# Two-layer graph network on one core: index copies on ScalarE, messages written by columns, 16-bit destination blocks

## The chip, the core and the metric

The kernel runs on one core of a Trainium2 chip. The metric is the device time of one execution in microseconds (us). The engines are PE (matmul), PEld (its weight loads), DVE (VectorE), ACT (ScalarE), POOL (GpSimd) and SP (SyncE, which here only issues DMAs). All 16 DMA engines serve all queues.

## The reference

There are 12500 nodes with 32 features and 200000 edges sorted by destination. Cut to what matters:

```python
# layer 0: a message per edge, summed over the edges of a destination
xs = concat(x[src, :8], x[dst, :8]); xv = concat(x[src, 8:], x[dst, 8:])      # 16 scalars, 16 3-vectors
h = 2.0 ** 0.5 * relu(emb @ W1 / 10.0 ** 0.5)
w = (h @ W2 / 16.0 ** 0.5).reshape(E, 7, 16, 8)                               # weights of each edge
s_out, g_out, v_out = (einsums of xs, xv, the edge's direction, and w)        # 8, 8 and 8x3
message = concat(G * tanh(s_out), G * tanh(g_out)[:, :, None] * v_out) * norm  # 32 numbers, G = 1.593
x = layernorm(x + segment_sum(message, dst))
# layer 1: attention over the edges of each destination
e = leaky_relu((x @ a1)[src] + (x @ a2)[dst])
x = layernorm(x + segment_sum(x[src] * softmax_by_dst(e), dst))
```

## The kernel before

Edges lie on 125 partitions, 1600 to each (EP = 1600), so a column is 125 edges. The kernel has three large stages and short ones between and behind them.

**The first stage (0 to about 378 us)** finds where each node's edges begin and end in the sorted list of destinations. The destinations come in as int32 (dst_i); DVE casts them to f32 (L332, dstf) and ACT stores them to DRAM as dstf_d, 500 blocks of 400 (L455 and the lines about it). A coarse search compares each node's number with the first entry of every block (L361 on DVE, L464 on ACT). For the fine search POOL gathers, for each of the 100 nodes of a partition, the right block of 400 destinations into one of NF = 8 buffers of blkbuf (L302, an indirect DMA), and DVE counts the entries that are at most the node's number (L381, one tensor_scalar with an accumulator). POOL may issue gather k when L381 has finished k - 8. Before these, POOL waits for the permuted features xp in DRAM (DVE L354 and L355, then ACT's store), gathers one row per head of a partition (L281) and 32 columns of source rows early (L287); behind the block gathers come 8 more columns, one small gather (L306) and 100 scatters of node rows to xd_d (L312). The message stage starts when these have landed. SP in the meantime writes 25.6 MB of zeros to xd_d and loads the edges' vectors.

**The message stage (378 to 2584 us)** goes over the 1600 columns in 200 pieces of 8 (PW = 8), 5 pieces to a chunk of 40 columns, 10 pieces (RING) to a turn of the loop. POOL gathers the source rows of each column into edge (L628), ten pieces ahead: when ACT has finished high(p) (semaphore b_hi), the slot of piece p is free and the gathers of piece p + 10 go into it. As the loop's piece is a register, POOL first copies the 8 index columns from src_i to idx (L625), waits for its own copy, and issues 8 gathers with columns of idx. The first turn takes src_i itself.

Per piece DVE projects the vectors on the edge's direction (two L865, one L870), ACT's function high places the features for PE (three copies at L673 and L674, into HL), PE transposes them (L758), ACT copies the result out (L680, FT), PE computes the hidden layer (L783; ACT relu, L684) and three pairs of products (L763), and DVE multiplies them by the hidden layer (L880, six per piece, 1000 columns each). PE sums (L792), ACT copies out (L688, rt), PE transposes back (L803, Y_ps), ACT takes tanh (L692, th), and DVE's function post makes the messages: L894 (pa), L899 (pg, the gates), L900 (the 8 scalars into O), L903 (pb), and later, between the second and third multiply of a step, L906 (the 24 vector entries into O). O is stored feature by feature, each of the 32 features with 41 columns (C1 = 41), because four scans over columns (L921) sum it by destination. pb lies as column, then 24 entries; pg as column, then 8; th as column, then 16. Each group of 4 columns is a step; the order of all these on an engine is written out by hand in the functions turn. Four more scans (L851) spread node rows over the edges, and ACT copies them in and out (L648, L660, L666). SP loads a chunk's inputs and stores its sums.

**The second layer (2780 to 4340 us)** looks rows up by one-hot matmuls on PE and by gathers on POOL. Two lines of DVE outside of the message stage serve as yardsticks: L1119 subtracts two tables of 26 x 33 entries, one of which it reads with 33 words from element to element while it writes runs; L1422 multiplies 40 rows of 32 and writes them 41 words apart.

```python
ov = cols(O[h])[:, 1 + c0:1 + c0 + PW, :]
V.tensor_tensor(ov[:, :, 8:32].rearrange("p c (w a) -> p c w a", a=3), pbv,
                pgv.rearrange("p c (w a) -> p c w a", a=1).broadcast_to([P, PW, MO, 3]), ALU.mult)
```

Of the kernel before, what the change touches and what calls it, by code (L numbers as in the profile page):

```python
# [5 lines left out]
def gnn_resnorm_kernel(nc, x, src, dst, emb, vec, weight, W1, W2, attn, out):  # L6
    f32 = mybir.dt.float32
    f32r = mybir.dt.float32r
    i32 = mybir.dt.int32
# [84 lines left out]
    with ctx:  # L94
# [7 lines left out]
            return nc.dram_tensor(name, shape, dt, kind="Internal").ap()  # L102


        dstf_d = dram("dstf_d", (NSB, SB))
        end_d = dram("end_d", (N + 1, 1))
        xd_d = dram("xd_d", (E, DIM))
        sd_d = dram("sd_d", (E, 1))
# [39 lines left out]
        R_ps = ctx.enter_context(nc.psum_tensor("R_ps", [128, 512], f32))  # L148
        Y_ps = ctx.enter_context(nc.psum_tensor("Y_ps", [128, 512], f32))

        src_i = sb("src_i", [PG, EP], i32)
        idx = sb("idx", [PG, RING * PW], i32)
        edge = sb("edge", [PG, RING * PW * EW])
        edge_c = edge[:, :].rearrange("p (c f) -> p c f", f=EW)
# [11 lines left out]
        with ExitStack() as st:  # L166
# [2 lines left out]

            dst_i = sbt("dst_i", [P, EP], i32)  # L170
            dstf = sbt("dstf", [P, EP + 1])
            prev_i = sbt("prev_i", [P, 1], i32)
            keep = sbt("keep", [P, EP])
            dirv = sbt("dirv", [P, EP * 3])
# [12 lines left out]
            cnt = sbt("cnt", [P, NP])  # L187
            blk_i = sbt("blk_i", [PG, NP], i32)
            fine = sbt("fine", [P, NP])
            blkbuf = sbt("blkbuf", [PG, NF * SB])  # L190
            w2s = sbt("w2s", [HID, 7 * 128])
            zeros = sbt("zeros", [PG, ZW])
            w2x = sbt("w2x", [HID, NR * MO * NQ * KF])
# [17 lines left out]
            with nc.Block() as block:  # L211
                @block.sync
                def _(sp):
                    by_rows(sp, dst_i[:, :], edges(dst, 1), S("a_dst"))
                    sp.wait_ge(S("a_idxz"), 2)
                    by_rows(sp, src_i[0:P, :], edges(src, 1), S("a_src"))
                    sp.dma_start(prev_i[1:P, :], dst.rearrange("(p c) -> p c", c=EP)[0:P - 1, EP - 1:EP], allow_slow_non_contiguous=True).then_inc(S("a_prev"), 16)
                    sp.wait_ge(S("a_zero"), 1)
                    sp.wait_ge(S("a_tab"), 32)
                    for i in range(NZ):  # L220
                        sp.dma_start(xd_d.rearrange("e f -> (e f)").rearrange("(p w) -> p w", p=PG)[:, i * ZW:(i + 1) * ZW], zeros[:, :]).then_inc(S("a_xd0"), 16)
                    sp.dma_start(end_d[0:1, :], zeros[0:1, 0:1]).then_inc(S("a_end"), 16)
                    sp.dma_start(w2s[:, :], W2).then_inc(S("a_w"), 16)
                    sp.dma_start(attn_b[:, :], attn.rearrange("(a f) -> a f", a=1).broadcast_to([P, 2 * DIM])).then_inc(S("a_w"), 16)
                    sp.wait_ge(S("a_wh0"), 1)
                    for row, k0, k1 in ((2 * KF + 8, 0, 8), (2 * KF + 24, 8, NEMB)):
                        sp.dma_start(w1x[row:row + k1 - k0, :].rearrange("k (w j) -> k w j", j=HID),
                                     W1[k0:k1, :].rearrange("k (w j) -> k w j", w=1).broadcast_to([k1 - k0, MO, HID])).then_inc(S("a_w1"), 16)
                    by_rows(sp, dirv[:, :], vec.rearrange("(p c) f -> p (c f)", c=EP), S("a_vec"))
                    sp.dma_start(sd_d.rearrange("e a -> (e a)").rearrange("(p w) -> p w", p=64), zeros[0:64, 0:E // 64]).then_inc(S("a_pad"), 16)  # L230
                    sp.dma_start(y0_d[E:E + PAD, :].rearrange("(a b) f -> a (b f)", a=64), zeros[0:64, 0:4 * DIM]).then_inc(S("a_pad"), 16)
                    sp.dma_start(y1_d[E:E + PAD, :].rearrange("(a b) f -> a (b f)", a=64), zeros[0:64, 0:4 * R1]).then_inc(S("a_pad"), 16)

                    sp.wait_ge(S("a_endf"), 1)
                    by_rows(sp, end_d[1:N + 1, :].rearrange("(p k) a -> p (k a)", k=NP), endf[:, :], S("a_end"))
                    sp.wait_ge(S("a_end"), 48)
                    by_rows(sp, startf[:, :], end_d[0:N, :].rearrange("(p k) a -> p (k a)", k=NP), S("a_start"))
                    sp.wait_ge(S("a_keep"), 1)
                    by_rows(sp, keep_d.rearrange("(p c) -> p c", c=EP), keep[:, :], S("a_out"))
                    sp.wait_ge(S("a_dir"), 1)  # L240
                    by_rows(sp, dir_d.rearrange("(p c) f -> p (c f)", c=EP), dirv[:, :], S("a_out"))
                    for a in range(2):
                        sp.wait_ge(S("a_selt"), a + 1)
                        sp.dma_start(sel_d[a].rearrange("(b r) p -> r b p", b=4), selT[a][:, :].rearrange("r (b p) -> r b p", b=4)).then_inc(S("a_out"), 16)
                    sp.wait_ge(S("a_out"), 96)
                    sp.wait_ge(S("a_pad"), 48)

                @block.gpsimd
                def _(pool):
# [47 lines left out]
                    for k in range(NP):  # L297
                        if k % NPH == 0:
                            pool.wait_ge(S("a_blk"), k // NPH + 1)
                        if k >= NF:  # L300
                            pool.wait_ge(S("a_fine"), k - NF + 1)
                        nc.gpsimd.indirect_dma_start(out=blkbuf[:, (k % NF) * SB:(k % NF + 1) * SB], out_offset=None, in_=dstf_d,  # L302
                                                     in_offset=bass.IndirectOffsetOnAxis(blk_i[:, k:k + 1], 0)).then_inc(S(f"a_fg{k % NF}"), 16)
                    early(EARLY - 1)
                    pool.wait_ge(S("a_start"), 32)
# [15 lines left out]
                def _(dve):  # L321
# [8 lines left out]
                    V.memset(zeros[:, :], 0.0).then_inc(S("a_zero"), 1)  # L330
                    dve.wait_ge(S("a_dst"), 32)
                    V.tensor_copy(dstf[:, 1:], dst_i[:, :]).then_inc(S("a_dstf"), 1)  # L332
                    dve.wait_ge(S("a_dstf"), 1)
                    dve.wait_ge(S("a_id"), 2)
                    V.tensor_tensor(blkbuf[0:P, 0:NSB].rearrange("p (j q) -> p j q", q=P),
# [41 lines left out]
                    for k in range(NP):  # L377
                        dve.wait_ge(S(f"a_fg{k % NF}"), 16 * (k // NF + 1))
                        if k >= NF:
                            dve.wait_ge(S("a_fine"), k - NF + 1)  # L380
                        V.tensor_scalar(junk[:, (k % NF) * SB:(k % NF + 1) * SB], blkbuf[0:P, (k % NF) * SB:(k % NF + 1) * SB], nodef[:, k:k + 1], None,  # L381
                                        ALU.is_le, ALU.add, accum_out=fine[:, k:k + 1]).then_inc(S("a_fine"), 1)
                    dve.wait_ge(S("a_fine"), NP)
                    V.scalar_tensor_tensor(endf[:, :], tn[:, 0:NP], float(SB), fine[:, :], ALU.mult, ALU.add).then_inc(S("a_endf"), 1)
# [55 lines left out]
                    step(V.tensor_copy(ssel[:, 0:E0], src_i[0:P, 0:E0]))  # L440
                    for pos in range(NB):
                        step(V.tensor_copy(ssel[:, E0:E0 + ITERS * XCB].rearrange("p (u c) -> p u c", c=XCB)[:, :, sum(XCS[:pos]):sum(XCS[:pos + 1])],
                                           src_i[0:P, :].rearrange("p (u h c) -> p u h c", h=NB, c=C)[:, :, pos, CGS[pos]:C]))
                    step(V.tensor_scalar(psel[:, :], ssel[:, :], 1.0 / KL, -(KL - 1) / (2.0 * KL), ALU.mult, ALU.add))
                    step(V.tensor_scalar(psel[:, :], psel[:, :], MAGIC, None, ALU.add))
                    V.tensor_scalar(psel[:, :], psel[:, :], -MAGIC, None, ALU.add).then_inc(S("a_sel"), 1)
# [3 lines left out]
                @block.scalar  # L450
                def _(act):
                    by_rows(act, xn[:, :], x.rearrange("(p k) f -> p (k f)", k=NP), S("a_x"))
                    act.wait_ge(S("a_dstf"), 1)
                    act.sem_inc(S("go"), 1)
                    by_rows(act, dstf_d.rearrange("a b -> (a b)").rearrange("(p c) -> p c", c=EP), dstf[:, 1:], S("a_dstd"))  # L455
                    act.wait_ge(S("a_xp"), 2)
                    act.sem_inc(S("go"), 1)
                    by_rows(act, xp_d.rearrange("(p k) f -> p (k f)", k=NP), xp[0:P, :], S("a_tab"))
# [38 lines left out]
        with ExitStack() as st:  # L497
# [58 lines left out]
            with nc.Block() as block:  # L556
# [51 lines left out]
                def _(pool):  # L608
# [8 lines left out]
                    def turn(t):  # L617
                        fixed = isinstance(t, int)
                        for s in range(RING):
                            p = t * RING + s  # L620
                            for c in range(PW):
                                pace(p, c)
                                i = s * PW + c
                                if c == 0 and not fixed:
                                    nc.gpsimd.tensor_copy(idx[:, i:i + PW], src_i[:, bass.ds((p + RING) * PW, PW)]).then_inc(S("b_ix"), 1)  # L625
                                    hold(S("b_ix"), p - RING + 1)
                                col = src_i[:, (p + RING) * PW + c:(p + RING) * PW + c + 1] if fixed else idx[:, i:i + 1]
                                nc.gpsimd.indirect_dma_start(out=edge_c[:, i, 8:8 + DIM], out_offset=None, in_=xp_d,  # L628
                                                             in_offset=bass.IndirectOffsetOnAxis(col, 0)).then_inc(S(f"b_gx{s}"), 16)
# [9 lines left out]
                def _(act):  # L639
# [25 lines left out]
                            act.wait_ge(S("b_st"), ch * 32)  # L665
                        A.activation(zr[:, :].rearrange("p (c f) -> p c f", f=DIM)[:, :, i * 8:(i + 1) * 8], cols(Z[h])[:, 1:, i * 8:(i + 1) * 8], ACT.Copy).then_inc(S("b_zr"), 1)  # L666

                    def high(p, s, ch):
                        act.wait_ge(S("b_al"), p + 1)
                        if s % PC == 0:  # L670
                            act.wait_ge(S("b_em"), ch * 2 + 2)
                        for d in range(2):
# [22 lines left out]
                    def turn(t, first=False, last=False):  # L695
                        for g in range(G2):
# [3 lines left out]
                                out_of_R(t * RING + g // 2 - 2)  # L700
                            if k == 0 and not (last and g + 4 >= G2):
                                s = (g + 4) // 2
                                high(t * RING + s, s % RING, t * 2 + s // PC)
                            if not (last and h == 1):
                                if gc == 0:
                                    place_emb(ch + 1, 1 - h, t + h)
# [130 lines left out]
                def _(dve):  # L837
# [48 lines left out]
                    def post(i, m, h, q, t):  # L886
                        c0 = q * PW
                        nrm = nmp[h][:, c0:c0 + PW].rearrange("p (c w) -> p c w", w=1).broadcast_to([P, PW, MO])
                        ov = cols(O[h])[:, 1 + c0:1 + c0 + PW, :]
                        if i == 0:  # L890
                            if q == 0:
                                dve.wait_ge(S(f"b_lp{h}"), t * 96 + 96)
# [4 lines left out]
                            if some(m):  # L897
                                dve.wait_ge(S("b_o"), m)
                            V.scalar_tensor_tensor(pgv, thv[:, :, 8:16], TG, nrm, ALU.mult, ALU.mult).then_inc(S("b_gs"), 1)  # L899
                            V.scalar_tensor_tensor(ov[:, :, 0:8], thv[:, :, 0:8], TG, nrm, ALU.mult, ALU.mult).then_inc(S("b_gs"), 1)  # L900
                        if i == 1:
                            dve.wait_ge(S("b_pa"), m + 1)
                            V.tensor_tensor(pbv, pav, yv[:, :, KF:KF + 24].rearrange("p c (a w) -> p c w a", a=3), ALU.add).then_inc(S("b_yr"), 1)  # L903
                        if i == 2:
                            dve.wait_ge(S("b_yr"), m + 1)
                            V.tensor_tensor(ov[:, :, 8:32].rearrange("p c (w a) -> p c w a", a=3), pbv,  # L906
                                            pgv.rearrange("p c (w a) -> p c w a", a=1).broadcast_to([P, PW, MO, 3]), ALU.mult).then_inc(S("b_o"), 1)

                    def carry_sums(ch, h, t):
                        if not isinstance(t, int) or t + h > 0:  # L910
# [663 lines left out]
```

## Time and profile before

| | us |
|---|---|
| median of 3 runs (lowest, highest) | 4478.09 (4477.6, 4480.03) |
| the profiled execution's own time | 4480.86 |
| its span | 4479.1 |
| first stage, from the span's start to | 378 |
| message stage | 378 to 2584 |
| between the layers | 2584 to 2780 |
| second layer | 2780 to 4340 |
| last sums and normalization | 4340 to 4479 |

The span reaches from the first to the last instruction; 1.8 us of the execution lie outside it. Idle time in the views is listed with what ended it. A line's mean is over instructions of one form where the view says "by form".

### The profile page before, as it was taken

The page shows a single profiled execution, that of the slowest core. Times are in us where ns is not written, and L with a number is a line of the kernel's source. Part 1 is how long each engine was busy: PE and PEld are TensorE (multiplying, and loading weights), DVE is VectorE, ACT ScalarE, POOL GpSimd, SP SyncE. Part 2 cuts the span into 40 slices and gives each one's busy share as a digit, 9 for nine tenths or more (in the row PEclk, how much of TensorE's full clock was granted, in tenths as well). Part 3 has the DMA queues.
Part 4 walks back from the last instruction along what each step waited for, and adds up shares of the span by engine and source line. Part 5 has one row for each costly group of instructions (what it writes and reads, how often), then busy time and mean ns, then how long its engine had stood idle before and what let it go on. Part 6 is the DMA issues. An engine that isn't in the chain of part 4 may idle for free. (4 is left out here: it accounts for less than half of the span.)

```text
span 4479.1 us, 67002 instructions
## 1 busy us (share of the span) xinstructions
PE 3332.8 (74%) x20487; PEld 2103.2 (47%) x20487; DVE 3036.9 (68%) x5225; ACT 2154.7 (48%) x4565; POOL 3247.6 (73%) x3440
## 2 busy tenths in 40 slices
PE   0003888888888888888888802999999999999940
PEld 0001332332332333233323202899999999999940
DVE  4433999999999999999999833344444444444432
ACT  3002555555555555555555310466666666666620
POOL 5776777777777777777777467777777777777766
PEclk9999999999999999999999955999999999999975
DMA  9612222222222222222222112133333333333311
GB/s 334 164 45 45 40 47 49 52 46 47 46 46 47 50 53 47 46 47 46 47 49 52 22 29 56 39 68 77 73 82 74 75 72 73 72 73 72 73 30 26
DMA packets 271192, 283.33 MB, mean 63 GB/s; under 512 B 182593, under 2 KB 236073, under 8 KB 268403
## 3 DMA queue, kind: packets, MB, share of 16 engines
q1 hardware_dynamic: 164150, 207.75, 16.8%
q0 software_dynamic: 106528, 70.98, 10.3%
q10 hardware_dynamic: 462, 4.00, 0.3%
q8 instruction: 21, 0.34, 0.0%
q14 instruction: 31, 0.25, 0.0%
HBM read 192.06 MB, written 90.42 MB: 63 GB/s over the span
## 5 line engine op out<-in xcount | busy, mean ns | idle before, releaser
L628 POOL DMA_INDIRECT edge<-xp_d,idx x1440 | 1420.8, 987 | 537.5 <-issue 393.6
L880 DVE TENSOR_TENSOR prod<-G_ps,hid 128x1000 f32<-128x1000 f32 x1200 | 1399.9, 1194 | 125.6 <-PE G_ps L763 111.3
L1275 POOL DMA_INDIRECT x1e<-tab_d,idxb x1122 | 1100.0, 980 | 342.2 <-issue 337.9
L763 PE MATMUL G_ps<-FT,wst 32*128 32x500 f32 x4800 | 896.6, 633 | 371.0 <-DVE prod L880 367.8
L1324 PE MATMUL G_ps<-tb,hot 128*126 128x442 f32 (+1 forms) x3968 | 799.1, 358 | 0.3 <-DVE x1e L1349 0.2
L1324 PEld LDWEIGHTS G_ps<-tb,hot 128*126 128x126 f32 x3968 | 743.0, 187 | 37.8 <-DVE x1e L1349 1.4
L763 PEld LDWEIGHTS G_ps<-FT,wst 32*128 32x128 f32 x4800 | 246.3, 183 | 807.4 <-DVE prod L880 750.7
L792 PE MATMUL R_ps<-prod,red 128*32 128x500 f32 x4800 | 590.5, 595 | 0.0
L684 ACT ACTIVATE hid<-T_ps 128x500 f32<-128x500 f32 x400 | 233.5, 584 | 721.5 <-PE T_ps L783 688.9
L1324 PE MATMUL T_ps<-tb,hot 128*126 128x442 f32 x2000 | 416.2, 360 | 186.3 <-DVE one_d L1408 186.3
L1324 PEld LDWEIGHTS T_ps<-tb,hot 128*126 128x126 f32 x2000 | 376.6, 188 | 204.9 <-issue 186.4
L783 PE MATMUL T_ps<-FT,wst 32*128 32x500 f32 x800 | 432.3, 619 | 3.1 <-ACT FT L680 3.1
L1349 DVE TENSOR_REDUCE x1e<-G_ps 125x17 f32<-125x442 f32 x496 | 269.9, 597 | 196.9 <-PE G_ps L1324 191.7
L758 PE MATMUL T_ps<-ident,HL 125*128 125x125 f32 x1600 | 250.1, 279 | 130.0 <-ACT HL L674 129.9
L1295 ACT ACTIVATE sqb<-x1e,sqb 125x32 f32<-125x32 f32 x1560 | 336.9, 341 | 0.0
L1324 PE MATMUL R_ps<-tb,hot 128*126 128x442 f32 x840 | 310.9, 370 | 16.9 <-DVE x1e L1349 16.9
L673 ACT ACTIVATE HL<-edge 125x384 f32<-125x384 f32 x400 | 187.3, 515 | 276.3 <-DVE edge L870 276.2
L792 PEld LDWEIGHTS R_ps<-prod,red 128*32 128x32 f32 x4800 | 115.6, 109 | 414.0 <-issue 266.3
L758 PEld LDWEIGHTS T_ps<-ident,HL 125*128 125x128 f32 x1600 | 177.3, 142 | 282.5 <-issue 149.9
L1324 PE MATMUL Y_ps<-tb,hot 128*126 128x416 f32 x840 | 300.0, 357 | 0.0
L1040 ACT ACTIVATE ab<-edge,niot 128x1375 f32<-128x1375 f32 (+2 forms) x172 | 245.4, 1451 | 74.1 <-PE Y_ps L1324 35.9
L1290 ACT ACTIVATE sqb<-ex 125x40 f32<-125x40 f32 x40 | 9.5, 239 | 527.9 <-DVE one_d L1381 527.9
(235 smaller groups left out, 4369.5 us busy)
## 6 DMA issues: line engine op xcount, KB each, us to landing
xd_d<-zeros SPq DMA_DIRECT2D x16, 1562.5 KB, 28.6
y_d<-ng SPq DMA_DIRECT2D x40, 595.0 KB
edge<-xp_d,idx POOLq DMA_INDIRECT x1440
xv<-xd_d SPq DMA_DIRECT2D x40, 560.0 KB
y_d<-zr SPq DMA_DIRECT2D x40, 560.0 KB
x1e<-tab_d,idxb POOLq DMA_INDIRECT x1122
edge<-sel_d SPq DMA_DIRECT2D x20, 750.0 KB
edge<-sel_d SPq DMA_DIRECT2D x20, 687.5 KB
```

The lines of the kernel that those rows point to most:

```text
L628: nc.gpsimd.indirect_dma_start(out=edge_c[:, i, 8:8 + DIM], out_offset=None, in_=xp_d, in_offset=bass.IndirectOffsetOnAxis(col, 0)).then_i ...
L684: A.activation(hid[k][:, :], T_ps[1][:, 0:GW], ACT.Relu, scale=HSCALE).then_inc(S("b_hid"), 1)
L758: last = Tn.transpose(T_ps[0][:, c * P:(c + 1) * P], HL[g // 2 % 2][:, col0:col0 + HW], ident[0:P, 0:P])
L763: return Tn.matmul(G_ps[pair][:, a * 512:a * 512 + GW], wst[rows, r * 128:(r + 1) * 128], FT[k][rows, :], start=True, stop=True)
L783: Tn.matmul(T_ps[1][:, 0:GW], wst[2 * KF:3 * KF, 128:256], FT[k][2 * KF:3 * KF, :], start=True, stop=True).then_inc(S("b_H"), 1)
L792: last = Tn.matmul(R_ps[32 * q:32 * q + 32, 0:GW], red[:, u * KF:(u + 1) * KF], prod[b * 2 + q // 2][pair][:, a * GW:(a + 1) * GW], start= ...
L880: V.tensor_tensor(prod[b][i][:, :].rearrange("p (a e) -> p a e", a=2), gv, hid[k][:, :].rearrange("p (a e) -> p a e", a=1).broadcast_to([1 ...
L1040: nc.scalar.activation(ab[g % 2][:, 0:w], nodek[b][:, 0:w] if g == NG4 - 1 else nodes[b][:, 0:w], ACT.Abs, bias=niot[:, g:g + 1]).then_inc ...
L1275: nc.gpsimd.indirect_dma_start(out=gx[b][:, c * T1:(c + 1) * T1], out_offset=None, in_=tab_d, in_offset=bass.IndirectOffsetOnAxis(idx[b][: ...
L1295: last = nc.scalar.activation(wxv[:, 1 + c, 0:DIM], gx[h][0:P, c * T1:c * T1 + DIM], ACT.Copy, scale=wx[:, DIM * C1 + 1 + c:DIM * C1 + 2 + c])
L1324: last = nc.tensor.matmul(ps[0:PE2, 0:w], hot[b][:, g * XPM + j * P:g * XPM + j * P + PE2], tb[l][:, g * GS + f0 * KL:g * GS + f0 * KL + w ...
L1349: V.tensor_reduce(gx[b][0:P, c * T1 + f0:c * T1 + f1], ps[0:P, 0:(f1 - f0) * KL].rearrange("p (f k) -> p f k", k=KL), AX.X, ALU.max).then_ ...
```

## The change

POOL no longer copies index columns. ACT does it in high, after its wait for DVE's projection and before its own three copies, for the pieces whose gathers the loop issues; POOL's wait for b_hi covers it. src_i is 16 columns wider, since ACT in its last full turn copies two pieces beyond the end. The two DVE instructions that write O run feature by feature with the columns innermost. In the first stage a second cast makes int16 destinations (dst16), they are what is stored and gathered (blk16), and DVE compares them in that form; blkbuf remains for the coarse search and two small tables.

```diff
-        dstf_d = dram("dstf_d", (NSB, SB))
+        dst16_d = dram("dst16_d", (NSB, SB), mybir.dt.int16)
...
-        src_i = sb("src_i", [PG, EP], i32)
+        src_i = sb("src_i", [PG, EP + 2 * PW], i32)
...
-            blkbuf = sbt("blkbuf", [PG, NF * SB])
+            blkbuf = sbt("blkbuf", [PG, 8 * P])
+            blk16 = sbt("blk16", [PG, NF * SB], mybir.dt.int16)
...
-                        nc.gpsimd.indirect_dma_start(out=blkbuf[:, (k % NF) * SB:(k % NF + 1) * SB], out_offset=None, in_=dstf_d,
+                        nc.gpsimd.indirect_dma_start(out=blk16[:, (k % NF) * SB:(k % NF + 1) * SB], out_offset=None, in_=dst16_d,
...
                     V.tensor_copy(dstf[:, 1:], dst_i[:, :]).then_inc(S("a_dstf"), 1)
+                    V.tensor_copy(dst16[:, :], dst_i[:, :]).then_inc(S("a_dstf"), 1)
...
-                        V.tensor_scalar(junk[:, (k % NF) * SB:(k % NF + 1) * SB], blkbuf[0:P, (k % NF) * SB:(k % NF + 1) * SB], nodef[:, k:k + 1], None,
+                        V.tensor_scalar(junk[:, (k % NF) * SB:(k % NF + 1) * SB], blk16[0:P, (k % NF) * SB:(k % NF + 1) * SB], nodef[:, k:k + 1], None,
...
-                    act.wait_ge(S("a_dstf"), 1)
+                    act.wait_ge(S("a_dstf"), 2)
                     act.sem_inc(S("go"), 1)
-                    by_rows(act, dstf_d.rearrange("a b -> (a b)").rearrange("(p c) -> p c", c=EP), dstf[:, 1:], S("a_dstd"))
+                    by_rows(act, dst16_d.rearrange("a b -> (a b)").rearrange("(p c) -> p c", c=EP), dst16[:, :], S("a_dstd"))
...
-                                if c == 0 and not fixed:
-                                    nc.gpsimd.tensor_copy(idx[:, i:i + PW], src_i[:, bass.ds((p + RING) * PW, PW)]).then_inc(S("b_ix"), 1)
-                                    hold(S("b_ix"), p - RING + 1)
...
-                    def high(p, s, ch):
+                    def high(p, s, ch, fetch=False):
                         act.wait_ge(S("b_al"), p + 1)
+                        if fetch:
+                            A.activation(idx[:, s * PW:(s + 1) * PW], src_i[:, bass.ds((p + RING) * PW, PW)], ACT.Copy)
...
-                                high(t * RING + s, s % RING, t * 2 + s // PC)
+                                high(t * RING + s, s % RING, t * 2 + s // PC, not last and not (first and s < RING))
...
-                        ov = cols(O[h])[:, 1 + c0:1 + c0 + PW, :]
+                        of = O[h][:, :].rearrange("p (f c) -> p f c", c=C1)[:, :, 1 + c0:1 + c0 + PW]
...
-                            V.scalar_tensor_tensor(ov[:, :, 0:8], thv[:, :, 0:8], TG, nrm, ALU.mult, ALU.mult).then_inc(S("b_gs"), 1)
+                            V.scalar_tensor_tensor(of[:, 0:8, :], thv[:, :, 0:8].rearrange("p c w -> p w c"), TG,
+                                                   nmp[h][:, c0:c0 + PW].rearrange("p (w c) -> p w c", w=1).broadcast_to([P, MO, PW]),
+                                                   ALU.mult, ALU.mult).then_inc(S("b_gs"), 1)
...
-                            V.tensor_tensor(ov[:, :, 8:32].rearrange("p c (w a) -> p c w a", a=3), pbv,
-                                            pgv.rearrange("p c (w a) -> p c w a", a=1).broadcast_to([P, PW, MO, 3]), ALU.mult).then_inc(S("b_o"), 1)
+                            V.tensor_tensor(of[:, 8:32, :].rearrange("p (w a) c -> p w a c", a=3), pbv.rearrange("p c w a -> p w a c"),
+                                            pgv.rearrange("p c (w a) -> p w a c", a=1).broadcast_to([P, MO, 3, PW]), ALU.mult).then_inc(S("b_o"), 1)
```

## Rows read from the trace of the kernel before

**Rows 1.** The page, busy us of the whole span.

```profile
PE 3332.8 (74%) x20487; PEld 2103.2 (47%) x20487; DVE 3036.9 (68%) x5225; ACT 2154.7 (48%) x4565; POOL 3247.6 (73%) x3440
```

**Rows 2.** Windows: stretch, length, busy us of each engine, PEclk, DMA share, GB/s.

```profile
378.00:2584.00 2206.00, 1808.71 (x12800) 656.96 (x12800) 2060.16 (x3207) 1144.81 (x2361) 1583.03 (x1740) 1.00 0.23 47
...
70.80:122.40 51.60, 0.00 (x0) 0.00 (x0) 11.09 (x35) 0.00 (x0) 22.66 (x24) 1.00 0.99 326
122.40:217.00 94.60, 0.00 (x0) 0.00 (x0) 50.03 (x161) 0.00 (x0) 71.72 (x76) 1.00 0.61 166
```

**Rows 3.** Waits, 1000 to 2000 us: total us, times, longest us.

```profile
PEld G_ps L763 <- DVE prod L880: 365.6, 365, 1.4
ACT hid L684 <- PE T_ps L783: 312.8, 145, 4.4
...
POOL edge L628 <- POOL idx L625: 70.7, 90, 0.8
...
DVE prod L880 <- PE G_ps L763: 41.4, 105, 1.0
```

**Rows 4.** One line: xcount, ns min/median/max, first and last start us; last row, L865's waits.

```profile
L302 POOL DMA_INDIRECT blkbuf<-dstf_d,blk_i x100: 943/949/963, 70.8 to 216.4; - x100
...
L381 DVE TENSOR_SCALAR_CACHE_REDUCE junk<-blkbuf,nodef x100: 625/629/631, 79.5 to 219.5; 125x400 bf16<-125x400 f32 x100
...
L625 POOL COPY idx<-src_i x174: 196/202/831, 601.4 to 2524.8; 128x8 int32 x174
...
L906 DVE TENSOR_TENSOR O<-pb,pg x184: 498/509/585, 609.4 to 2579.5; 125x192 f32<-125x192 f32 x184
...
  DMA edge<-xp_d,idx: 1.0, 1
```

**Rows 5.** Timeline, message stage: start us, length us, engine, line.

```profile
1512.84 0.26 ACT L692 ACTIVATE th<-Y_ps 125x128 f32<-125x128 f32 x1
...
1513.72 0.35 DVE L894 TENSOR_TENSOR pa<-Y_ps,drp 125x192 f32<-125x192 f32 x1
...
2535.00 0.94 POOL L628 DMA_INDIRECT edge<-xp_d,idx  x1 [0.30 <-issue]
```

**Rows 6.** Timeline, first stage: in brackets the idle time before.

```profile
12.81 1.00 DVE L332 CAST dstf<-dst_i 125x1600 f32<-125x1600 int32 x1 [8.60 <-DMA dst_i<-in_dst]
...
27.86 1.39 POOL L281 DMA_INDIRECT hx_keep<-xp_d,head_i  x1 [18.70 <-DMA xp_d<-xp]
...
201.35 0.95 POOL L302 DMA_INDIRECT blkbuf<-dstf_d,blk_i  x1 [0.30 <-DVE junk L381]
```

**Rows 7.** ACT by line and form, 560 to 4479 us: busy us, mean ns.

```profile
L1290 ACT ACTIVATE sqb<-ex 125x40 f32<-125x40 f32 x40 | 9.5, 239 | 527.9 <-DVE one_d L1381 527.9
```

**Rows 8.** DVE by line and form, 560 to 4479 us: busy us, mean ns.

```profile
L880 DVE TENSOR_TENSOR prod<-G_ps,hid 128x1000 f32<-128x1000 f32 x1115 | 1300.8, 1194 | 102.6 <-PE G_ps L763 89.6
...
L870 DVE TENSOR_REDUCE edge<-tmp 125x128 f32<-125x384 f32 x183 | 105.5, 576 | 1.3
L906 DVE TENSOR_TENSOR O<-pb,pg 125x192 f32<-125x192 f32 x188 | 96.9, 515 | 0.1
...
L903 DVE TENSOR_TENSOR pb<-pa,Y_ps 125x192 f32<-125x192 f32 x188 | 65.1, 346 | 0.0
...
L900 DVE SCALAR_TENSOR_TENSOR O<-th,nmp 125x64 f32<-125x64 f32 x188 | 50.8, 270 | 0.0
L899 DVE SCALAR_TENSOR_TENSOR pg<-th,nmp 125x64 f32<-125x64 f32 x188 | 40.8, 217 | 0.0
...
L1119 DVE TENSOR_TENSOR tb<-tbl,tb 128x858 fp32r<-128x858 f32 x4 | 6.6, 1697 | 17.4 <-ACT tb L1151 17.4
...
L1422 DVE TENSOR_TENSOR sqb<-x1e,sqb 125x1280 f32<-125x1280 f32 x1 | 2.5, 2464 | 0.0
```

**Rows 9.** DMA queues, 80 to 90 us: packets, MB, share of 16 engines.

```profile
q1 hardware_dynamic: 298, 3.33, 78.6%
q0 software_dynamic: 294, 0.91, 22.5%
```

More of the change, by code:

```diff
@@ L171, in gnn_resnorm_kernel @@
             dstf = sbt("dstf", [P, EP + 1])
+            dst16 = sbt("dst16", [P, EP], mybir.dt.int16)
             prev_i = sbt("prev_i", [P, 1], i32)
@@ L215, in _ @@
                     sp.wait_ge(S("a_idxz"), 2)
-                    by_rows(sp, src_i[0:P, :], edges(src, 1), S("a_src"))
+                    by_rows(sp, src_i[0:P, 0:EP], edges(src, 1), S("a_src"))
                     sp.dma_start(prev_i[1:P, :], dst.rearrange("(p c) -> p c", c=EP)[0:P - 1, EP - 1:EP], allow_slow_non_contiguous=True).then_inc(S("a_prev"), 16)
@@ L442, in _ @@
                         step(V.tensor_copy(ssel[:, E0:E0 + ITERS * XCB].rearrange("p (u c) -> p u c", c=XCB)[:, :, sum(XCS[:pos]):sum(XCS[:pos + 1])],
-                                           src_i[0:P, :].rearrange("p (u h c) -> p u h c", h=NB, c=C)[:, :, pos, CGS[pos]:C]))
+                                           src_i[0:P, 0:EP].rearrange("p (u h c) -> p u h c", h=NB, c=C)[:, :, pos, CGS[pos]:C]))
                     step(V.tensor_scalar(psel[:, :], ssel[:, :], 1.0 / KL, -(KL - 1) / (2.0 * KL), ALU.mult, ALU.add))
```

## The prediction

> **What bounds the kernel now.** I began with the page [rows 1]: over the whole span PE, DVE and POOL are each busy about 70%, which is a mean over stages with different limits. So I cut the span into stages [rows 2]. The message stage (378 to 2584 us, half of the run) is the one the change mostly edits: DVE is busy 2060 of 2206 us, 93%, while PE has 82%, POOL 72% and ACT 52%. The table of waits says what the other 7% is [rows 3]: in 1000 us DVE waited 41 us for PE's G_ps, and PE waits for DVE many times longer. DVE's own work sets this stage.
>
> The share of POOL misleads, though. From 600 us on, its index copy starts first at 601.4 and, 173 copies later, at 2524.8 [rows 4]: 11.12 us per piece of 8 columns. DVE's L906, also once per piece, goes from 609.4 to 2579.5 in 183 steps: 10.77 us. POOL is slower than DVE by 0.35 us per piece and lives off its lead of ten pieces. The lead is just used up at the end: the last gather issues at 2535.0 [rows 5], and DVE waits for gathered rows once, 1.0 us [rows 4]. POOL is at the edge of being the bound, and costs 1 us now.
>
> The first stage ends with POOL too. One queue runs through it: early gathers, 100 gathers of destination blocks (70.8 to 216.4 [rows 4]), then 100 scatters; the message stage begins behind them. Where nothing holds it up, a block gather costs POOL 0.95 us plus 0.30 before the next [rows 6], 1.25 us; 99 steps want 124.2 us and took 145.6, so 21.4 us are stalls. They lie before 122.4, where the DMA engines are 99% busy; later they are 61% busy and POOL runs at its own pace [rows 2].
>
> **The change part by part, and the sum.**
>
> *Index copies, POOL to ACT.* Off POOL go 180 copies with the wait behind each: 0.20 us [rows 4] plus 70.7/90 = 0.79 us [rows 3], about 1 us per piece. POOL then needs some 10.1 us and waits for ACT's HL instead; no one waits for POOL. Worth: the 1.0 us at the end. ACT gets 180 copies of 8 columns. Nearest row: 239 ns for 40 columns [rows 7]; I take 0.2 us for 8, bounds 0 and 0.24. Each stands after the wait for DVE's L870 and ahead of HL, so everything queued behind it (HL, the copies of ds or xv, tanh, relu) starts 0.2 us later. The tightest cover I found is tanh to L894 in a piece with ds copies: tanh starts at 1512.84 for 0.26 us, L894 at 1513.72, 0.6 us to spare [rows 5]. Relu's own start is set by PE (313 us of waits in 1000 [rows 3]), which leaves ACT room ahead of it. I put it at 0; with the cover gone it would be up to 180 x 0.24 = 43 us. POOL's copies sharing SBUF with DVE: L906's mean is 515 and its median 509 [rows 4, 8], so their end is worth 0 to 1 us; I take 0. Nothing moves to or from SP's queue.
>
> *Messages along the columns.* Now L900 and L906 write O with a step of 41 words per element and read in runs. After it they write runs of 8 columns, and the reads step: L906 reads pb every 24 words and pg every 8, L900 reads th every 16 (nmp in a run). What do such steps cost? Two DVE rows without any (L880 with 1000 elements in 1194 ns, L903 with 192 in 346) give 1.05 ns per element and 144 ns fixed [rows 8]. A strided write, from the same rows: L906 is 169 ns above L903 of the same size, 0.88 per element; L1422 (1280 elements, writes 41 words apart) is 976 ns above the line, 0.76. A strided read: L1119 reads one of its two sources 33 words apart and writes in runs; 858 elements should take 1045 ns and take 1697, so 0.76 per element. A far step thus costs the same on a read as on a write, and the edit exchanges one for the other. With one such charge L906 becomes 346 + 192 x 0.76 = 492 ns, 23 less, x 200 pieces = -4.6 us. L900 becomes 217 + 64 x 0.76 = 266, 4 less; it stands where DVE next waits for PE, so 0. Between multiply 1 and multiply 2, where L906 stands, DVE doesn't wait, so it counts in full.
>
> Both of L906's sources step, however, and no row has that. Lower end: steps on reads almost free. L870 reads 384 elements 8 words apart in 576 ns against 547 by the line, 0.08 per element; so 361 ns, -154, -31 us. Upper end: two charges add, 346 + 2 x 0.76 x 192 = 638 ns, +123, +24.6 us. I take one charge, since L1119 is nearest (two sources, DVE, SBUF) and L870 has but one source.
>
> The Trainium skill's "Vector Engine (DVE) Microarchitecture Reference", section 5.2, speaks against this edit: two sources hopping per element cost little more than one (1.76 against 1.73 ns per column), but both stepping 24 words cost 2.50. The first figure agrees with the 1.81 of L1119; by the second, L906 would be an estimated 624 ns and the edit would lose 22 us. Rival A has that outcome with a price from rows.
>
> *16-bit destination blocks.* Each gather brings 128 rows of 800 B instead of 1600. DVE issues one more cast, ahead of the coarse search and of xp; L332, the same cast to f32, is 1.0 us [rows 6]. It lies ahead of everything up to xp, which DVE works off without a gap that could hide it, and POOL's queue starts at 27.86, when xp_d has landed [rows 6]; so +1.0, bounds 0.5 to 1.8, and behind it POOL and the whole stage shift. ACT's store of the blocks waits for the second cast too, but is not needed before 70.8, and halved it gets out of xp_d's way. The comparison L381 (629 ns [rows 4]) fits within POOL's 1.25 at either width: 0. Steady pace doesn't change either, since POOL sets it.
>
> The gain is in the 21.4 us of stall. From 80 to 90 us q1 (the zeros) and q0 (the gathers) take turns, 298 and 294 packets, 11.2 and 3.1 KB each [rows 9]. Halving the small packet of such a pair shortens it by 1.5 of 14.3 KB, about 10%; were there also fewer packets, it would be up to half. By bytes alone, q0's share of 22.5% would halve. Both ends: 0 and 21.4; I take a third, 7 to 8 us. Less the cast: -7.
>
> Sum: -7 (first stage), -4.6 (L906), -1.0 (POOL's wait) = -12.6. The profiled execution took 4480.9, 1.8 of it outside the span; it becomes 4468.3. The median of the runs is 2.8 below it, so 4478.1 - 12.6 = **4465.5 us**.
>
> **The rivals.**
>
> A, other side: the two strided reads of L906 add up, 638 ns. +24.6 - 7 - 1 = +16.6, 4494.7. For: pb and pg are distinct SBUF sources, both step at every element, and a writing step alone already costs 0.88. Against: only that no row shows it. Break-even is +40 ns (L906 at 555); from 600 ns it is slower by over 0.2%.
>
> B: reads in this order are cheap, 361 ns. -31 - 7 - 1 = -39, 4439. For: L870. Against: L1119. Only here does POOL's relief matter: at 11.12 us per piece it couldn't follow, at 10.1 it can.
>
> C: the 16-bit blocks don't shorten the stalls, because packets and not bytes are what takes turns. +1 - 4.6 - 1 = -4.6, 4473.5: the edit does not do what it says.
>
> D: ACT's copy shows up in DVE's waits for tanh. +20 to +43 on top, about 4500.
>
> **How the numbers follow.** Forecast 0.36, A 0.30, B 0.14, C 0.14, D 0.06. About 0.2% (9 us, 4469 to 4487) is what a measurement of this kernel can tell from no change. Faster: three quarters of the forecast's case, B, and a little of C = 0.43. Same: the rest of the forecast, most of C, a tail of A = 0.23. Slower: A and D = 0.34. The range goes from B, 4440, to just beyond A, 4500; with cases of both signs, the likeliest one's own range is 4455 to 4474 (stall gain 0 to 18).
>
> **What would show it.** L906 at about 490 ns, L900 near 266: right; 600 or more: A; below 400: B. The block gathers' span 138 us instead of 145.6, start 1.0 later. No L625; POOL idle before L628 named ACT HL, some 0.6 us per piece; DVE's waits for edge gone, and for tanh still below 10 us. Piece pace 10.75 instead of 10.77. The forecast is wrong if L906 is more than 40 ns above 515, or if the scatters begin no earlier.

## The result and the profile after

The changed kernel takes 4507.85 us (4501.05 to 4509.06) against 4477.85: 30.0 us more, ratio 1.0063, 95% interval 1.0048 to 1.0078. I forecast 12.6 us less. Times are medians; one execution of e12 below ran in a slower state of the chip (5017 us) and is left out of its median. The two profiled executions, stage by stage, by the first or last instruction of each stage:

| stretch | before, us | after, us | difference |
|---|---|---|---|
| to POOL's first gather of the message stage | 378.6 | 370.4 | -8.2 |
| message stage, to DVE's last copy (2583.1, 2605.2) | 2204.5 | 2234.8 | +30.3 |
| from there to L1119/L1123 (2763.7, 2785.8) | 180.6 | 180.6 | 0 |
| second layer, to the last gathers' start (4337.5, 4365.3) | 1573.8 | 1579.5 | +5.7 |
| the rest | 141.6 | 141.1 | -0.5 |

The first stage gained what was forecast and the message stage lost more than all of it. The 5.7 us of the second layer stand in code that nobody edited; over all the kernels of this study that stretch took 1573.8 to 1580.7 us, without a pattern, and I don't count it.

The windows of the kernel after (length, busy us of PE, PEld, DVE, ACT, POOL, PE clock, DMA share, GB/s), to be read beside [rows 2]:

```profile
71.70:115.00 43.30, 0.00 (x0) 0.00 (x0) 12.10 (x38) 0.00 (x0) 25.52 (x27) 1.00 0.97 333
115.00:210.00 95.00, 0.00 (x0) 0.00 (x0) 49.60 (x158) 0.00 (x0) 69.09 (x74) 1.00 0.33 86
370.00:2606.00 2236.00, 1803.94 (x12800) 656.14 (x12800) 2102.65 (x3203) 1162.05 (x2543) 1560.80 (x1560) 1.00 0.23 46
```

DVE is still the busy engine of the message stage, 2103 of 2236 us. The lines of DVE by form (total and mean ns; line numbers have moved: L910 is L906 of before, L902 is L900, L907 is L903, L901 is L899, L872 is L870, L882 is L880), beside [rows 8]:

```profile
L882 DVE TENSOR_TENSOR prod<-G_ps,hid 128x1000 f32<-128x1000 f32 x1112 | 1295.3, 1192 | 94.4 <-PE G_ps L765 78.0 <-issue 1.0
...
L910 DVE TENSOR_TENSOR O<-pb,pg 125x192 f32<-125x192 f32 x188 | 114.4, 609 | 0.1
...
L872 DVE TENSOR_REDUCE edge<-tmp 125x128 f32<-125x384 f32 x183 | 105.3, 575 | 1.3
...
L907 DVE TENSOR_TENSOR pb<-pa,Y_ps 125x192 f32<-125x192 f32 x187 | 64.2, 344 | 0.0
...
L902 DVE SCALAR_TENSOR_TENSOR O<-th,nmp 125x64 f32<-125x64 f32 x187 | 47.7, 255 | 0.0
L901 DVE SCALAR_TENSOR_TENSOR pg<-th,nmp 125x64 f32<-125x64 f32 x187 | 40.5, 217 | 0.0
```

L910 takes 609 ns for 515, L902 255 for 270; the rest stands. In durations that is 200 x (94 - 15) ns = 16 us, half of the 30. The other half is seen only in the timeline (start us, length us, engine, line). Before:

```profile
1506.95 0.55 DVE L906 TENSOR_TENSOR O<-pb,pg 125x192 f32<-125x192 f32 x1
1507.34 1.18 DVE L880 TENSOR_TENSOR prod<-G_ps,hid 128x1000 f32<-128x1000 f32 x1
```

After:

```profile
1505.65 0.61 DVE L910 TENSOR_TENSOR O<-pb,pg 125x192 f32<-125x192 f32 x1
1506.18 1.19 DVE L882 TENSOR_TENSOR prod<-G_ps,hid 128x1000 f32<-128x1000 f32 x1
```

DVE starts its next instruction before the last one has ended, so an instruction's length is not what it costs. What it costs is the time to the next start, here called its slot: 0.39 us for L906 in this piece, 0.53 for L910. I took the mean over some 146 pieces from 700 to 2300 us: L906 0.347, L910 0.526; L900 0.137, L902 0.173. L902 is shorter than L900 and occupies DVE longer. Over 200 pieces the longer slot of L910 makes 200 x 0.179 = 35.8 us and that of L902 another 7. DVE was busy 42.5 us longer in the stage, and the stage grew by 30.3: part of the work fell into waits and gaps that DVE had before (see L900 below).

The waits of 1000 us (total us, times, longest), beside [rows 3]:

```profile
PEld G_ps L765 <- DVE prod L882: 381.8, 364, 1.5
...
ACT idx L671 <- DVE edge L872: 151.4, 91, 1.8
...
POOL edge L628 <- ACT HL L676: 47.9, 64, 1.4
DVE prod L882 <- PE G_ps L765: 35.9, 95, 1.0
```

POOL's wait for its own copies is gone and it waits for ACT's HL now, 0.5 us per piece. ACT's copy, in high, and the block gathers with what they waited for:

```profile
L671 ACT ACTIVATE idx<-src_i x182: 208/209/211, 487.0 to 2477.0; 128x8 int32 x180, 128x8 int32<-128x8 int32 x2
```

```profile
L304 POOL DMA_INDIRECT blk<-dst_d,blk_i x100: 942/946/962, 71.7 to 208.7; - x100
...
  DVE junk L384: 19.0, 19
```

The block gathers span 137.0 us (forecast: 138) and start 0.9 later (forecast: 1.0); POOL's waits for L384, the comparison that frees a buffer, add up to 19.0 us, where before it waited 41.8 for L381. The queues from 80 to 90 us, beside [rows 9]:

```profile
q1 hardware_dynamic: 323, 3.54, 84.5%
q0 software_dynamic: 323, 0.68, 17.4%
```

q0 still gets packets through one for one with q1, but smaller ones, 2.1 KB for 3.1.

### The profile page after: what moved, and what is told of

It reads as the page before. It is cut to its first block and busy times, and to the rows that moved or that the text cites. A ratio compares the mean times of both kernels' runs of the same rounds, so it can differ in the third digit from the quotient of the medians.

```text
span 4506.4 us, 66644 instructions
## 1 busy us (share of the span) xinstructions
PE 3326.6 (74%) x20487; PEld 2100.4 (47%) x20487; DVE 3079.3 (68%) x5226; ACT 2171.9 (48%) x4747; POOL 3225.4 (72%) x3260
## 5 line engine op out<-in xcount | busy, mean ns | idle before, releaser
L628 POOL DMA_INDIRECT edge<-xp_d,idx x1440 | 1441.8, 1001 | 499.9 <-issue 423.6
L882 DVE TENSOR_TENSOR prod<-G_ps,hid 128x1000 f32<-128x1000 f32 x1200 | 1397.7, 1192 | 117.5 <-PE G_ps L765 99.9
L1048 ACT ACTIVATE hot<-ab,ones 128x1375 fp32r<-128x1375 f32 (+2 forms) x172 | 243.8, 1441 | 0.0
```

Source lines behind the costliest of these rows:

```text
L882: V.tensor_tensor(prod[b][i][:, :].rearrange("p (a e) -> p a e", a=2), gv, hid[k][:, :].rearrange("p (a e) -> p a e", a=1).broadcast_to([1 ...
L1048: nc.scalar.activation(hot[b][:, g * XPM:g * XPM + w], ab[g % 2][:, 0:w], ACT.Relu, bias=ones[:, 0:1], scale=-1.0).then_inc(S("d_hot"), 1)
```

## The experiments

Theory 1: the whole loss is the column edit, and slots, not durations, carry it. Theory 2 is its rival of the run at hand: in e1 and e4 that ACT's index copies cost part of the loss, in e2 that durations count as they stand. Then, for L910's price: theory A, every source that steps is charged; theory S, the distance of the step decides. "Stage" is the message stage as in the table above. The runs were made on three chips (e1 to e4, e5 to e9, e10 to e13), where the kernel before had medians of 4477.8, 4477.9 and 4484.5 us. Each ratio is to the one of the same chip.

**One part at a time.** Kernel e1 is the changed kernel with L900 and L906 as they were:

```diff
...
-                            V.tensor_tensor(of[:, 8:32, :].rearrange("p (w a) c -> p w a c", a=3), pbv.rearrange("p c w a -> p w a c"),
-                                            pgv.rearrange("p c (w a) -> p w a c", a=1).broadcast_to([P, MO, 3, PW]), ALU.mult).then_inc(S("b_o"), 1)
+                            V.tensor_tensor(ov[:, :, 8:32].rearrange("p c (w a) -> p c w a", a=3), pbv,
+                                            pgv.rearrange("p c (w a) -> p c w a", a=1).broadcast_to([P, PW, MO, 3]), ALU.mult).then_inc(S("b_o"), 1)
...
```

> The changed kernel with L900 and L906 written as before. Theory 1, the whole loss lies in the column edit: L906 (here L906/L908) back at 515 ns, the message stage back at about 2204 us, first stage 8 us shorter than before, so about 4469 us, 9 below the kernel before. Theory 2, the index copy on ACT costs part of the message stage's 30 us: about 4480 us, the stage near 2215 us.

Measured: 4471.14 us, ratio 0.998 (0.9971 to 0.9989), stage 2199.8. L906 and L900 (here L908, L902) are back:

```profile
L908 DVE TENSOR_TENSOR O<-pb,pg 125x192 f32<-125x192 f32 x187 | 95.0, 508 | 0.1
...
L902 DVE SCALAR_TENSOR_TENSOR O<-th,nmp 125x64 f32<-125x64 f32 x187 | 50.5, 270 | 0.0
```

The loss is gone, so it lay in the column edit. Against e1 that edit costs 36.7 us in the medians and 35.0 in the stage. L906's slot is 0.337 us in e1, so L910's 0.526 costs 37.8 us more over the 200 pieces. The stage is even 4.7 us shorter than before.

Kernel e2 is the kernel before with the column edit alone (the same lines, the other way).

> The kernel before with the column edit alone. Theory 1: message stage 2235 us, about 4508 us, 30 above before, though L906 is only 94 ns longer and L900 15 ns shorter (200 x 0.079 = 16 us). Theory 2, durations count as they stand: 16 us above before, about 4494 us.

Measured: 4514.3 us, ratio 1.0077 (1.0061 to 1.0092), stage 2234.7; 36.5 us above before:

```profile
L908 DVE TENSOR_TENSOR O<-pb,pg 125x192 f32<-125x192 f32 x188 | 114.5, 609 | 0.1
```

Theory 2, the sum of durations (16 us), falls; theory 1 forecast 30 and got the size.

Kernel e3 has the 16-bit blocks alone:

```diff
-        dstf_d = dram("dstf_d", (NSB, SB))
+        dst16_d = dram("dst16_d", (NSB, SB), mybir.dt.int16)
...
```

> The kernel before with 16-bit destination blocks alone. Both theories: the message stage starts 8 us earlier (370.4 for 378.6), about 4470 us. If POOL's queue in the message stage was the second bound, its last gather issues 8 us earlier too, and the gain is kept.

Measured: 4471.34 us, ratio 0.9987 (0.9978 to 0.9997). The message stage starts at 370.1, 8.5 us earlier, and takes 2201.2; its last gather issues at 2523.2 for 2535.0, and the gain is kept. Over all the kernels here the stage starts at 369.0 to 371.2 us with the 16-bit blocks and at 377.1 to 378.6 without.

Kernel e4 has the index copies on ACT alone:

```diff
-                    nc.gpsimd.tensor_copy(idx[:, i:i + PW], src_i[:, bass.ds((p + RING) * PW, PW)]).then_inc(S("b_ix"), 1)
-                    hold(S("b_ix"), p - RING + 1)
...
+                    A.activation(idx[:, s * PW:(s + 1) * PW], src_i[:, bass.ds((p + RING) * PW, PW)], ACT.Copy)
```

> The kernel before with the index copies on ACT alone. Theory 1: within 2 us of before, 4477 us, since POOL cost only 1.0 us at the end and ACT has 0.6 us to spare. Theory 2: up to 14 us slower, 4490 us, with more waits of DVE for tanh or G_ps.

Measured: 4474.93 us, ratio 0.9993 (0.9984 to 1.0002), stage 2198.7. The waits of DVE in the message stage:

```profile
DVE prod L879 <- PE G_ps L762: 110.9, 243, 8.0
...
DVE pa L893 <- ACT th L691: 6.5, 3, 3.8
```

Before:

```profile
DVE prod L880 <- PE G_ps L763: 111.3, 239, 7.9
...
DVE pa L894 <- ACT th L692: 7.8, 3, 4.3
```

ACT's 0.21 us per piece shows nowhere. Theory 2 is out. In its profile the stage is 5.8 us shorter, in the medians 2.9 us with an interval that takes in zero. e1 and e3, which differ in the index copies alone, have 4471.14 and 4471.34 us, stages of 2199.8 and 2201.2: the copies are worth nothing or a little. What can be seen of it is in DVE: L906's slot is 0.337 us in e1 and e4, 0.344 in e3 and 0.347 before, which makes 1 to 2 us over 200 pieces.

**What L910 pays for.** Kernels e5 and e6 only pad the columns of pb (and in e5 of pg), so that the reads step by another distance:

```diff
-            pb = sbt("pb", [P, PW * 24])
+            pb = sbt("pb", [P, PW * 25])
...
```

> The changed kernel with pb's columns 25 words apart instead of 24 and pg's 9 instead of 8; every read of L910 still steps. Theory A, each source that steps is charged alike: L910 stays at 609 ns, 4508 us. Theory S, the size of the step decides (24 or 8 words is a bad one, the 33 of L1119 a better one): L910 falls to about 490 ns and the time by 200 x 0.12 = 24 us to 4484 us.

> As e5, but only pb at 25 words; pg stays at 8. Theory A: 609 ns. Theory S with pb's 24 words as the bad step: about 490 ns, 4484 us; with pg's 8 words as the bad one: 609.

Measured: e5 4497.91 us, ratio 1.0046 (1.0031 to 1.0061), L910 558 ns; e6 4497.06 us, ratio 1.0041 (1.0025 to 1.0056), stage 2224.5, with this L910:

```profile
L910 DVE TENSOR_TENSOR O<-pb,pg 125x192 f32<-125x192 f32 x187 | 104.5, 559 | 0.1
```

One word more between pb's columns takes off 50 ns; pg's 8 or 9 words make no difference. The distance of pb's step matters, though 559 is not the 490 of theory S.

Kernel e8 stores pg column innermost, so that one source steps and the other runs:

```diff
-                            V.scalar_tensor_tensor(pgv, thv[:, :, 8:16], TG, nrm, ALU.mult, ALU.mult).then_inc(S("b_gs"), 1)
+                            V.scalar_tensor_tensor(pgw, thv[:, :, 8:16].rearrange("p c w -> p w c"), TG,
+                                                   nmp[h][:, c0:c0 + PW].rearrange("p (w c) -> p w c", w=1).broadcast_to([P, MO, PW]),
+                                                   ALU.mult, ALU.mult).then_inc(S("b_gs"), 1)
...
```

> The changed kernel with the gates pg stored column innermost (L901 reads th with steps and writes runs), so that L910 reads pg in runs and only pb steps, by 24. Theory A: one charge less, L910 about 490 ns, L901 up from 217 to 256 ns; about 4495 us. Theory S, pb's 24 words: L910 stays near 609, and the time rises a little, to about 4512 us.

Measured: 4503.13 us, ratio 1.0054 (1.0038 to 1.0069), stage 2235.8. L910 (here L912) doesn't move:

```profile
L912 DVE TENSOR_TENSOR O<-pb,pg 125x192 f32<-125x192 f32 x188 | 114.4, 608 | 0.1
...
L901 DVE SCALAR_TENSOR_TENSOR pg<-th,nmp 125x64 f32<-125x64 f32 x187 | 47.3, 253 | 0.0
```

Theory A falls: pg's steps of 8 words cost nothing beside pb's of 24. Two sources that both step far were not run.

Kernels e11 and e12 put pb's columns 33 and 32 words apart.

> The changed kernel with pb's columns 33 words apart, pg at 8. If the price goes by the size or residue of the step and L1119 (33 words, 0.76 ns per element) holds for L910: 344 + 146 = 490 ns, the message stage 2211 us. If L910's two sources cost more than L1119's one: 559 ns as with 25 words, 2224 us.

> As e11 with 32 words. If multiples of 8 words are the bad steps, as 24 against 25 suggests: 609 ns and a stage of 2235 us. If only the distance matters, between 24, 25 and 33: about 500 ns.

Measured: e11 4488.35 us, ratio 1.0008 (0.9998 to 1.0018), stage 2213.6; e12 4488.58 us, ratio 1.0004 (0.9994 to 1.0015), stage 2212.4. L910 in e11, then in e12:

```profile
L910 DVE TENSOR_TENSOR O<-pb,pg 125x192 f32<-125x192 f32 x188 | 95.1, 506 | 0.1
```

```profile
L910 DVE TENSOR_TENSOR O<-pb,pg 125x192 f32<-125x192 f32 x187 | 94.9, 507 | 0.1
```

So it isn't multiples of 8 that are bad. Above an L907 of 344 ns the price per element is 1.38 ns at 24 words, 1.12 at 25, 0.85 at 32 and 0.84 at 33. Why it falls with the distance I can't tell from these.

**The steps taken off L910.** Kernel e9 stores pa, pb and pg all column innermost. L910 reads and writes runs; the steps go to Y_ps in PSUM, to drp, and to th.

```diff
-            pav = pa[:, :].rearrange("p (c w a) -> p c w a", w=MO, a=3)
-            pbv = pb[:, :].rearrange("p (c w a) -> p c w a", w=MO, a=3)
-            pgv = pg[:, :].rearrange("p (c w) -> p c w", w=MO)
+            pav = pa[:, :].rearrange("p (w a c) -> p w a c", w=MO, a=3)
+            pbv = pb[:, :].rearrange("p (w a c) -> p w a c", w=MO, a=3)
+            pgw = pg[:, :].rearrange("p (w c) -> p w c", w=MO)
...
```

> The changed kernel with pa, pb and pg all column innermost: L910 reads and writes runs; the steps go to PSUM reads (Y_ps, 64 words apart) and to drp (3 words) in L896 and L907. If PSUM steps are free as in L903 of before (8 words apart, 346 ns) and drp's steps are cheap: L910 346 ns, L907 346 ns, L896 350 to 490 ns; message stage 2170 to 2200 us, 4440 to 4470 us, below e1's 4471. If a PSUM read 64 words apart is charged like SBUF's: L896 and L907 each 490 ns or more and nothing is won, about 4500 us.

Measured: 4455.0 us, ratio 0.9952 (0.9939 to 0.9966), stage 2183.5. Its lines (L912 is L910, L909 is L907, L904 is L902):

```profile
L896 DVE TENSOR_TENSOR pa<-Y_ps,drp 125x192 f32<-125x192 f32 x187 | 77.9, 417 | 7.0 <-ACT th L694 7.0
...
L912 DVE TENSOR_TENSOR O<-pb,pg 125x192 f32<-125x192 f32 x187 | 65.0, 347 | 0.1
...
L909 DVE TENSOR_TENSOR pb<-pa,Y_ps 125x192 f32<-125x192 f32 x187 | 64.5, 345 | 0.0
...
L901 DVE SCALAR_TENSOR_TENSOR pg<-th,nmp 125x64 f32<-125x64 f32 x187 | 48.1, 257 | 0.0
L904 DVE SCALAR_TENSOR_TENSOR O<-th,nmp 125x64 f32<-125x64 f32 x187 | 47.1, 252 | 0.0
```

L912 is down to 347 ns, and L909 is unmoved at 345 though its PSUM source now steps 64 words per element. L896 takes 69 ns more; both its sources step now, Y_ps by 64 words and drp by 3, and since the first cost L909 nothing I put the 69 ns down to drp. L912's slot, in one piece:

```profile
1500.42 0.35 DVE L912 TENSOR_TENSOR O<-pb,pg 125x192 f32<-125x192 f32 x1
1500.69 1.19 DVE L882 TENSOR_TENSOR prod<-G_ps,hid 128x1000 f32<-128x1000 f32 x1
```

The stage is 16.3 us below e1's; L912's slot fell from 0.337 to 0.266, which is 14.2 us. The slots of L896, L901 and L904 together rose by 0.14 us, 28 us in sum, and it doesn't show: behind them DVE waits for PE's G_ps, and that wait shrank from 110 to 62 us. (The view leaves out waits under about 0.15 us, so such sums don't balance to the microsecond.)

Kernel e10 puts the steps of L901 and L904 on the writes:

```diff
-                            V.scalar_tensor_tensor(pgw, thv[:, :, 8:16].rearrange("p c w -> p w c"), TG,
...
+                            V.scalar_tensor_tensor(pgw.rearrange("p w c -> p c w"), thv[:, :, 8:16], TG, nrm, ALU.mult, ALU.mult).then_inc(S("b_gs"), 1)
...
```

> As e9, but L901 and L904 read th in runs and write with steps (8 and 41 words); L912 is unchanged. Start to next start, e9 has 0.173 and 0.168 us for the two, and a stepping write had 0.137 before. Theory, a step on a write hides behind the next instruction and one on a read doesn't: durations rise to about 265 ns, the slots fall to 0.137. In total 0.067 us x 200 = 13 us less work; where DVE waits for PE behind them it gives nothing, so 4455 to 4442 us, likely 4450. If durations were what counts: a little slower than e9.

Measured: 4456.36 us, ratio 0.9937 (0.9923 to 0.995), stage 2182.7:

```profile
L901 DVE SCALAR_TENSOR_TENSOR pg<-th,nmp 125x64 f32<-125x64 f32 x187 | 51.0, 273 | 0.0
L902 DVE SCALAR_TENSOR_TENSOR O<-th,nmp 125x64 f32<-125x64 f32 x187 | 50.0, 267 | 0.0
```

Both are longer than in e9 (273 for 257, 267 for 252) and both have the shorter slot, 0.135 us each for 0.173 and 0.168. The claim about slots holds; the time doesn't move. DVE's wait for PE in e9, then in e10:

```profile
DVE prod L882 <- PE G_ps L765: 61.8, 99, 7.9
```

```profile
DVE prod L882 <- PE G_ps L765: 93.0, 223, 7.9
```

That wait takes the 14 us back. Its 31 us are more than that because many of e9's gaps were too short to be listed: counted from start to start, with the waits in them, the scans and the line that writes pb (L909, here L905) rose by 14 us in sum. The ratios of e9 and e10 agree within their intervals, and both are below the kernel before and the changed one.

Kernel e13 is e9 with the index copies on POOL again.

> e9 with the index copies on POOL again. POOL then needs 11.1 us per piece against DVE's 10.7. Theory, POOL becomes the bound at the end of its lead: its last gather issues about 2527 us and the message stage ends some 45 us later, near 2573 instead of 2554; about 4473 us, with DVE waits for edge<-xp_d of some 15 to 20 us. Rival, the lead still lasts: 4457 us and no such waits.

Measured: 4457.45 us, ratio 0.9939 (0.9924 to 0.9955), stage 2185.0; no wait of DVE for gathered rows is listed. POOL's copy:

```profile
L628 POOL COPY idx<-src_i x180: 196/202/882, 523.4 to 2487.1; 128x8 int32 x180
```

179 steps from 523.4 to 2487.1 are 10.97 us each, not 11.1: the mean gather takes 970 ns, where it took 987 before. DVE's L913 comes every 10.66 us, so POOL loses 0.31 us per piece, where it lost 0.35 before, and the lead lasts: its last gather issues 58 us ahead of the stage's end, before 48. The rival was right: even in the fastest form POOL's relief isn't needed.

## Why the prediction was wrong

The sum was -12.6 us; the medians say +30.0, outside of the range, and rival A's 4494.7 was too low as well. By its own steps:

- **L906, forecast -4.6 us, measured about +35.** This is the step that failed, "a far step thus costs the same on a read as on a write, and the edit exchanges one for the other". It failed twice. The price: I took L1119's 0.76 ns per element, of a step of 33 words, for one of 24, which costs 1.38; with 33 words in L910 itself it is 0.84 (e11). And the currency: I compared lengths. In e1 the stepping write is 161 ns longer than the run of e9 but its slot is only 0.071 us longer (0.337 against 0.266), the rest of its extra length lying under the next instruction. A stepping read of 33 words is 159 ns longer and its slot grows by 0.155 (0.421). So the exchange would have lost even at the price I took: e11 lies 13.8 us above e1 in the stage. L910 stands where DVE doesn't wait, and its slot alone accounts for the stage in all the forms, to 3 us; what the lines ahead of a wait gained or lost (28 us in e9) went into the wait:

| kernel | L910's slot, us | 200 x (slot - 0.266) | stage - 2183.5 |
|---|---|---|---|
| e9, runs | 0.266 | 0 | 0 |
| e1, writes step 41 words | 0.337 | 14.2 | 16.3 |
| e12, reads step 32 | 0.424 | 31.6 | 28.9 |
| e11, reads step 33 | 0.421 | 31.0 | 30.1 |
| e6, reads step 25 | 0.476 | 42.0 | 41.0 |
| after, reads step 24 | 0.526 | 52.0 | 51.3 |
| e8, pb steps 24, pg in runs | 0.526 | 52.0 | 52.3 |

- **L900, forecast 0.** Right in time and for the reason given. The cost I had wrong: I had it 4 ns shorter, and its slot grew by 0.036 us. DVE's wait for PE behind it shrank (in 1000 us from 41.4 to 35.9).
- **Rival A** had the sign and nearly the length (638 forecast, 609 measured) by a mechanism that e8 speaks against: pg's charge doesn't add to pb's, one source stepping 24 words pays it all. Its +24.6 us for L906 counts lengths; the slots make it 35.8. Rival B took L870's near-free steps of 8 words for L906's. They were no guide; whether the distance, the single source or the reduce makes L870 cheap no run here shows.
- **16-bit blocks, forecast -7.** The stage start moved by -8.2, gathers' span 137.0 us, start +0.9 (e3 alone: -8.5 and 6.4 in the medians). Rival C is out: the stalls did shrink, by 8.6 us. (My 124.2 us for the unhindered gathers is 123.8 by its own 1.25 us; it changes nothing.)
- **Index copies, forecast -1.0.** e4 gives -2.9 with an interval that includes zero, e1 against e3 gives -0.2. ACT's copy took 0.209 us (0.2 forecast) and delayed nobody; rival D is out. That POOL was at the edge of being the bound was true of the one wait, but the edge was harmless (e13).

The Trainium skill's "Vector Engine (DVE) Microarchitecture Reference", section 5.2, gives about 2.50 ns per column where both sources step 24 words. With 1.05 ns per element for a run, L910 took 1.05 + (609 - 344) / 192 = 2.43 by its length and 1.05 + (526 - 266) / 192 = 2.40 by its slot: the trace agrees. That one source stepping 24 words costs as much as two (e8) the section has no figure for; it has the like for hops of 4 KiB. I had set its figure beside the sum, with the chance of a rival, because L1119 seemed nearer; it was nearer in kind, not in the step. And the section's figures are spans over 64 instructions back to back, so they count to the next start as the slots do. I had set them beside lengths.

## What to carry to other kernels

Where an engine starts its next instruction before the last has ended, cost an edit by the time to the next start, not by the instruction's length. Here a stepping write of 192 elements hid more than half of its extra 161 ns under the next instruction, one of 64 elements nearly all of its 54, and a stepping read none. Before moving a step from one operand to another, see whether the layouts between producer and consumer can take it off altogether, or put it where a row shows it free (here PSUM reads), as e9 did: 16 us of the message stage against e1, and 23 us in all, with the 16-bit blocks, against the kernel before. A price per element taken from another line is only good for the same distance of step.

## What was unexpected in the hardware

- The price of a stepping SBUF read in a two-source DVE instruction fell with the distance: 609 ns for 192 elements at 24 words, 559 at 25, 507 at 32, 506 at 33, 347 in runs. The cause stays open.
- L902 was 15 ns shorter than L900 and occupied DVE 0.036 us longer; L901 and L904 the same way round in e9 against e10. The length of an instruction can fall while its cost rises.
- A PSUM source stepping 64 words per element cost L909 nothing (345 ns).
- The mean gather on POOL (560 to 2480 us) went with the kernel around it, while its median stayed at 944 to 947 ns. With the index copies on POOL it was 970 ns in e13, 979 in e2 and 987 before; with the copies on ACT 981 in e9, 1001 in the changed kernel, 1009 in e1 and 1017 in e11. So each gather was 11 to 23 ns longer once the copies were on ACT. The cause stays open.
